# Two transformer layers in one kernel: zero rows by ScalarE, bias adds by GpSimd, and a reordered load queue

## The reference

```python
x = L0_attn_x                                # (4, 256, 512) f32
xn = _layernorm(x)
x = x + attn0(xn) + gelu(xn @ W1 + fc1_bias) @ W2 + fc2_bias             # hidden 2048
xn = _layernorm(x)
x1, x2 = split(xn @ w12.T + b12)                                         # hidden 512
x = x + causal_attn1(xn) + (silu(x1) * x2) @ w3.T + b3                   # 32 heads, 8 key heads of 16
```

## Time and profile before

| quantity | value |
| --- | --- |
| median of 3 runs (lowest, highest) | 619.87 us (619.39, 623.91) |
| the profiled execution | 624.43 us |
| its span, first to last instruction | 622.3 us |
| mean granted PE clock | 0.981 of full speed |
| first transpose, first maximum matmul, first score on PE | 9.70, 35.22 and 46.83 us into the span |
| ACT's first square root (L855) | 7.78 us |
| POOL's last memset or mask ends | 27.2 us |
| PE's wait ahead of the first up product | 25.7 to 29.4 us |
| DVE's last work ahead of 542 us ends | 540.0 us |
| layer 0 / layer 1 border (unit 16's first scores) | about 390 us |
| busy share of PE, DVE, ACT, POOL | 93%, 73%, 57%, 35% |
| bytes moved by DMA | 67.29 MB, 108 GB/s mean |

### The profile page before, as it was taken

One profiled execution on the slowest core, in us unless ns is written; L12 is line 12 of the kernel. 1 busy time (PEld: TensorE's weight loads), 2 busy tenths in 40 slices (PEclk: granted clock), 3 DMA queues, 4 the chain that ended last, 5 costly groups with the idle time before them and its releaser, 6 DMA issues.

```text
span 622.3 us, 10485 instructions
## 1 busy us (share of the span) xinstructions
PE 577.9 (93%) x3232; PEld 443.3 (71%) x3232; DVE 451.5 (73%) x1198; ACT 356.0 (57%) x611; POOL 217.8 (35%) x332
## 2 busy tenths in 40 slices
PE   2698899999999999999999998899989989899997
PEld 2686677787777878667777777677767877666754
DVE  6559967656566675576897677889997988578663
ACT  3337766755555683676694575657655654465541
POOL 5712423122303321211223122354644555254241
PEclk9999899999999999999999999989999999988989
DMA  5583542353223244315443332425433344334101
GB/s 186 176 241 127 141 115 67 105 153 103 68 86 103 70 131 124 86 45 160 120 136 101 95 90 74 120 85 139 141 98 102 86 127 130 87 102 116 23 5 63
DMA packets 29806, 67.29 MB, mean 108 GB/s; under 512 B 4788, under 2 KB 17588, under 8 KB 27704
## 3 DMA queue, kind: packets, MB, share of 16 engines
q1 hardware_dynamic: 21112, 38.32, 22.2%
q0 software_dynamic: 8640, 28.32, 15.6%
HBM read 51.67 MB, written 14.68 MB: 107 GB/s over the span
## 4 chain that ended last, share of the span: by engine, by line
PE 73%; DVE 9%; ACT 6%; issue 5%; DMA 5%; POOL 1%; SPq 1%; ACTq 0%; DVEq 0%; POOLq 0%
PE banks L692 49%; PE banks L745 8%; PE banks L771 7%; PE banks L793 7%; DMA q_sb<-q_parts 2%; DVE banks L1065 1%; DMA q_sb<-max_t 1%; ACT L910 1%; PE banks L774 1%; PE banks L712 1%; ACT hid_f L930 1%; ACT L929 1%; DVE bn L976 1%; ACT probs L910 1%; DVE x_res L1109 1%
## 5 line engine op out<-in xcount | busy, mean ns | idle before, releaser
L910 ACT ACTIVATE probs<-banks 128x512 f32<-128x512 f32 (+1 forms) x256 | 137.6, 545 | 185.1 <-PE banks L771 143.9
L692 PE MATMUL banks<-xnT,w_up 128*128 128x512 f32 x576 | 154.7, 403 | 5.4 <-issue 3.8
L1070 DVE TENSOR_REDUCE neg_max<-banks 128x2 f32<-128x512 f32 x128 | 87.1, 687 | 93.2 <-PE banks L745 92.6
L692 PE MATMUL banks<-w_down,hid 128*128 128x512 f32 x480 | 131.1, 407 | 4.5 <-ACT hid_f L930 2.0
L692 PEld LDWEIGHTS banks<-xnT,w_up 128*128 128x128 f32 x576 | 103.4, 192 | 33.9 <-issue 15.1
L1065 DVE CUSTOM_DVE_ANT_0 banks<-banks,mask_qk 128x128 f32<-128x128 f32 (+1 forms) x256 | 86.3, 374 | 39.4 <-PE banks L745 39.4
L692 PEld LDWEIGHTS banks<-w_down,hid 128*128 128x128 f32 x480 | 87.7, 193 | 32.3 <-DVE neg_max L1070 6.7
L745 PEld LDWEIGHTS banks<-k_sb,q_sb 96*128 96x128 f32 x512 | 93.7, 193 | 23.3 <-issue 5.2
L745 PE MATMUL banks<-k_sb,q_sb 96*128 96x256 f32 (+1 forms) x512 | 100.8, 279 | 5.2 <-DMA q_sb<-q_parts 4.0
L648 POOL TENSOR_SCALAR_AFFINE_SELECT probs<-probs 128x256 f32<-128x256 f32 x128 | 59.6, 466 | 102.6 <-ACT probs L910 97.5
L771 PE MATMUL banks<-q_sb,k_sb 97*128 97x512 f32 x192 | 79.9, 416 | 8.8 <-ACT probs L910 6.9
(11 more groups left out here) (77 smaller groups left out, 651.3 us busy)
## 6 DMA issues: line engine op xcount, KB each, us to landing
q_sb<-q_parts SPq DMA_DIRECT2D x64, 256.0 KB, 4.4
raw<-in_up POOLq DMA_DIRECT2D x48, 256.0 KB, 3.0
raw<-in_down POOLq DMA_DIRECT2D x40, 256.0 KB, 3.1
q_parts<-stage SPq DMA_DIRECT2D x32, 256.0 KB, 2.5
raw<-in_attn POOLq DMA_DIRECT2D x20, 256.0 KB, 3.2
k_parts<-stage SPq DMA_DIRECT2D x16, 256.0 KB, 2.6
k_sb<-k_parts SPq DMA_DIRECT2D x16, 256.0 KB, 4.0
x_res<-in_x SPq DMA_DIRECT2D x4, 512.0 KB, 4.0
```

Source lines behind the costliest of these rows:

```text
L692: mm = nc.tensor.matmul(out_ap, lhs(a), rhs(b_), start=first and j == 0, stop=stop and j == 2, **kw)
L910: nc.scalar.activation(probs[:, i, 0:w], banks[:, ST_BANKS[k % 2], 0:w], ACT.Exp, scale=SCALES[n // B]).then_inc(exp_done, 1)
L1070: nc.vector.tensor_reduce(neg_max[:, s, 2 * g:2 * g + 2, t], banks[:, bank_of[x], :].rearrange("p (r t) -> p r t", r=2)[:, :, 0:w], AX.X, ...
```

## The change

Six edits are made together.

1. POOL no longer zeroes q_sb; three ACT copies from a zero column do (`fill`). Two stand ahead of everything else on ACT, the third behind the second batch's transposes. POOL's other memsets are put in another order, and its raw loads no longer alternate with them.
2. The first batch of x is loaded as two DMAs of 256 KB, one for each tile.
3. The key loads (`load_k`) of batch 0 go behind the first query store on SP.
4. The three output biases are now laid out as 128 x 512 arrays each and loaded by three DMAs of 256 KB instead of two of 8 KB. POOL sums two of them once (`bias`).
5. The sixteen bias matmuls are gone. Sixteen POOL additions of bias_out to a tile of x_res (`plus`) take their place: six in unit 3, two in each of units 7, 11, 15, 19 and 23. The DVE additions of products to x_res stay.
6. Each `out` stands behind the next `mrow` instead of right behind the tile's last product.

```diff
 def start_slots():
-    o = [[("stats", 0, 0), ("root", 0, 0), ("rstd", 0, 0), ("ln", 0)] + split(0, "attn", 4, 5)]
+    o = [[("fill", 0), ("fill", 1), ("stats", 0, 0), ("root", 0, 0), ("rstd", 0, 0), ("ln", 0)] + split(0, "attn", 4, 5)]
     o += [[("xn", 0, 0), ("xn", 0, 1)] + split(0, "attn", 0, 1)]
...
     o += [parts(("qkv", 0, 2)) + split(0, "attn", 2, 3)]
-    o += [parts(("qkv", 0, 0)) + [("load_k", 0, 0), ("load_k", 0, 1)]]
-    o += [[("xn", 1, 0), ("xn", 1, 1), ("load_q", 0), ("load_q", 1)] + split(0, "up", 0, 1)]
+    o += [parts(("qkv", 0, 0))]
+    o += [[("xn", 1, 0), ("xn", 1, 1), ("fill", 2), ("load_k", 0, 0), ("load_k", 0, 1), ("load_q", 0), ("load_q", 1)] + split(0, "up", 0, 1)]
     o += [parts(("qkv", 0, 1)) + [("v", 0)]]
...
         slots[7].append(("rstd", 1, c))
+    if s == 3 and n + 2 < 2 * B:
+        for c in ((0, 1, 2) if n == 0 else (n + 2,)):
+            slots[2 if n else 2 * c].append(("plus", c // B, TT * (c % B)))
+            slots[4 if n else 2 * c + 1].append(("plus", c // B, TT * (c % B) + 1))
     if s == 2 and n + 2 < 2 * B:
...
         k = max(k for k, x in enumerate(o) if adds_to(x) == (1, tile))
-        o.insert(k + 1, ("out", tile))
+        rows = [j for j, x in enumerate(o) if j > k and x[0] == "mrow"]
+        o.insert((rows[0] if rows else k) + 1, ("out", tile))
     return o
...
         return x[1] // B, TT * (x[1] % B) + x[2]
+    if x[0] == "plus":
+        return x[1], x[2]
...
         bias_up = sb("bias_up", [P, 24])
-        bias_out = sb("bias_out", [P, 2, D], F32R)
-        ones = sb("ones", [P, P], F32R)
+        bias_out = sb("bias_out", [P, 2, D])
+        zero = sb("zero", [P, 1])
...
-        bias_raw = probs[:, 6:8, :]
+        bias_more = probs[:, 7, :]
...
 
-            eng.wait_ge(wk_emptied, em[x if x[0] == "wo" else ("down",) + x[1:]] + 1)
+            if x[0] == "plus":
+                eng.wait_ge(plus_done, pls[x] + 1)
+            else:
+                eng.wait_ge(wk_emptied, em[x if x[0] == "wo" else ("down",) + x[1:]] + 1)
 
...
 
-        IDENT, Q_ZERO, ONES_V, ZEROED, ALL_MADE, EARLY = 2, 7, 8, 9, 12, 9
+        IDENT, K_ZERO, ONES_V, ALL_MADE, EARLY = 3, 4, 5, 8, 4
 
...
 
-            load_x(0)
+            for t in range(TT):
+                sp_.dma_start(x_res[:, t, :], x_in[0][t * P:t * P + P, :]).then_inc(x_loaded[0] if t else x_first, 16)
             sp_.wait_ge(raw_loaded[1], 16)
...
                 if x[0] == "load_bias":
-                    sp_.wait_ge(made, ZEROED)
-                    for row in (0, 32):
-                        sp_.dma_start(bias_raw[row:row + 2, :, :], out_b).then_inc(bias_loaded, 16)
+                    for k, to in enumerate((bias_out[:, 0, :], bias_out[:, 1, :], bias_more)):
+                        sp_.dma_start(to, out_b[k]).then_inc(bias_loaded, 16)
                 if x[0] == "store":
...
 
+            nc.gpsimd.memset(zero[:, :], 0.0).then_inc(made, 1)
+            pool.wait_ge(made, 1)
             load(0)
...
             nc.gpsimd.memset(ident[:, :], 0.0).then_inc(made, 1)
-            pool.wait_ge(made, 1)
+            pool.wait_ge(made, 2)
             nc.gpsimd.affine_select(out=ident[:, :], in_=ident[:, :], compare_op=ALU.not_equal, fill=1.0,
...
             pool.wait_ge(made, IDENT)
+            nc.gpsimd.memset(k_sb[64:ROWS, :, :].bitcast(F32), 0.0).then_inc(made, 1)
+            pool.wait_ge(made, K_ZERO)
             pool.wait_ge(x_loaded[0], 16)
...
             load(3)
-            nc.gpsimd.memset(k_sb[64:ROWS, :, :].bitcast(F32), 0.0).then_inc(made, 1)
-            pool.wait_ge(made, 3)
-            load(4)
-            load(5)
-            nc.gpsimd.memset(k_sb[MROW:MROW + 1, :, :].bitcast(F32), 1.0).then_inc(made, 1)
-            pool.wait_ge(made, 4)
-            for k in range(RING):
-                load(6 + k)
-                nc.gpsimd.memset(q_sb[64:ROWS, k, :, :].bitcast(F32), 0.0).then_inc(made, 1)
-                pool.wait_ge(made, 5 + k)
             nc.gpsimd.memset(v_sb[:, :, :, :], 1.0).then_inc(made, 1)
             pool.wait_ge(made, ONES_V)
-            nc.gpsimd.memset(bias_raw[:, :, :], 0.0).then_inc(made, 1)
-            pool.wait_ge(made, ZEROED)
-            nc.gpsimd.memset(ones[:, :].bitcast(F32), 1.0).then_inc(made, 1)
-            pool.wait_ge(made, 10)
+            nc.gpsimd.memset(k_sb[MROW:MROW + 1, :, :].bitcast(F32), 1.0).then_inc(made, 1)
+            pool.wait_ge(made, ALL_MADE - 2)
             nc.gpsimd.memset(mask_qk[:, :], 0.0).then_inc(made, 1)
-            pool.wait_ge(made, 11)
+            pool.wait_ge(made, ALL_MADE - 1)
             nc.gpsimd.affine_select(out=mask_qk[:, P:], in_=mask_qk[:, P:], compare_op=ALU.is_ge, fill=MASKED,
...
                     done[0] = (mask_done, st_index(u - LU, i) + 1)
+                if x[0] == "bias":
+                    pool.wait_ge(bias_loaded, 48)
+                    in_order()
+                    nc.gpsimd.tensor_tensor(bias_out[:, 1, :], bias_out[:, 1, :], bias_more, ALU.add).then_inc(bias_summed, 1)
+                    done[0] = (bias_summed, 1)
+                if x[0] == "plus":
+                    _, L, tile = x
+                    n, t = B * L + tile // TT, tile % TT
+                    pool.wait_ge(ln_done, TT * n + t + 1)
+                    if add_before[x]:
+                        wait_tile_sum(pool, add_before[x])
+                    in_order()
+                    nc.gpsimd.tensor_tensor(x_res[:, tile, :], x_res[:, tile, :], bias_out[:, L, :], ALU.add).then_inc(plus_done, 1)
+                    done[0] = (plus_done, pls[x] + 1)
                 if x[0] == "ctx":
...
                     k = work(x)
-                    if x == ("m", 0, 0):
-                        pe.wait_ge(made, Q_ZERO)
+                    if u < RING and i == 0:
+                        pe.wait_ge(made, K_ZERO)
+                        pe.wait_ge(q_zeroed, u + 1)
                     if i == 0:
...
                     k = work(x) if opens else bank_of[x]
-                    if opens and rest == 0:
-                        pe.wait_ge(bias_split, 1)
-                        nc.tensor.matmul(banks[:, k, :], ones[:, :], bias_out[:, L, :],
-                                         start=True, stop=False, skip_group_check=True)
                     if opens:
...
                         mm = three(banks[:, k, :], lambda h: hid[:, c % HID, h, t * P:t * P + P],
-                                   lambda h: w_down[:, c % 2, h, :], rest > 0 and e == 0, e == 1, skip_group_check=True)
+                                   lambda h: w_down[:, c % 2, h, :], e == 0, e == 1, skip_group_check=True)
                     if closes:
...
                     nc.scalar.copy(to[0], raw[:, k % RAW, :]).then_inc(hi_split, 1)
+                if x[0] == "fill":
+                    act.wait_ge(made, 1)
+                    nc.scalar.copy(q_sb[64:ROWS, x[1], :, :].rearrange("p g t -> p (g t)"),
+                                   zero[64:ROWS, :].to_broadcast([ROWS - 64, UH * T])).then_inc(q_zeroed, 1)
                 if x[0] == "root":
...
                     act.wait_ge(st_filled, k + 1)
-                    if k == 6:
-                        act.wait_ge(bias_split, 1)
+                    if k == 7:
+                        act.wait_ge(bias_summed, 1)
                     if u:
...
                         if L == 0:
-                            dve.wait_ge(x_loaded[t // TT], 16)
+                            dve.wait_ge(x_loaded[t // TT] if t else x_first, 16)
                         else:
...
                                             ALU.add).then_inc(rot_done, 1)
-                if x[0] == "bias":
-                    dve.wait_ge(bias_loaded, 32)
-                    link(nc.vector.tensor_copy(bias_out[:, :, :], bias_raw[:, :, :]))
-                    nc.vector.tensor_tensor(bias_out[32:64, :, :], bias_raw[32:64, :, :],
-                                            bias_out[32:64, :, :].bitcast(F32), ALU.subtract).then_inc(bias_split, 1)
                 if x[0] == "v":
...
                         nc.vector.transpose(o_t[:, :], o_div[:, :]).then_inc(o_back, 1)
-                if adds_to(x):
+                if adds_to(x) and x[0] != "plus":
                     tile = adds_to(x)[1]
...
     up_b = np.concatenate([i["L0_ffn_fc1_bias"].reshape(-1, P), i["L1_ffn_b12"].reshape(-1, P)]).T
-    zero = np.zeros(D, np.float32)
-    out_b = np.stack([np.stack([i["L0_ffn_fc2_bias"], i["L1_ffn_b3"]]), np.stack([zero, i["L1_attn_b_dense"]])])
+    out_b = np.stack([np.broadcast_to(b, (P, D)) for b in (i["L0_ffn_fc2_bias"], i["L1_ffn_b3"], i["L1_attn_b_dense"])])
     inv = (np.float32(1.0) / np.power(np.float32(1e6), np.arange(0, HD, 2, dtype=np.float32) / np.float32(HD))).astype(np.float32)
```

6 lines of the change are left out of this document (5 added, 1 removed).

## The result

The changed kernel took **614.2 us** (median of four runs, 611.85 to 617.68) against 621.62 us for the kernel before, measured beside it (four runs, 619.39 to 623.91). The ratio is 0.9869, 95% interval 0.9833 to 0.9906: 1.3% faster, 8 us by the ratio (the two medians lie 7.4 us apart). Its profiled execution took 612.6 us, with a span of 610.8 us, 11.5 us shorter than the 622.3 us of before; 9.9 us were forecast for that pair. The two profiled executions differ in their clock too. Before had a mean granted clock of 0.981 and after one of 0.989, so full clock was withheld for 11.8 us of the first span (0.019 of 622.3) and 6.7 us of the second.

A forecast was written before the change was run, and what follows sets the result against it. PE, busy for 577.9 of 622.3 us, was taken to bound the kernel, apart from a few waits. Terms 2.9 + 1.0 + 2.4 + 3.0 + 0.6 - 1.5 gave 8.4 us, 611.5 us from 619.87, range 605 to 617.

The forecast's parts named there:

- The start: Up to the first maximum matmul: the query store moves up, gaining 2.9 us, bounds 0.5 and 5 us.
- the first rival: Start gives nothing back: wait moves ahead of the maxima, clock falls, bias loads delay the first row; 615.4 us, 22%.
- Unit 0: Bias operations off DVE gain 1.5 us, less 0.5 for the bias loads: net 1.0 us.
- the 0.5 for the bias loads: In unit 0, 768 KB of loads ahead of the first row of maxima: loss between 0 and 2 us, 0.5 taken.
- Bias matmuls: Sixteen fewer on PE at 0.23 us each, ten or eleven counted: 2.4 us gained, bounds 1.2 and 3.7.
- The stall: PE's wait and slow clock around 542 us end: 4.5 us in the profiled execution, 3.0 us in the median.
- The limit that I expected of DVE: At the stall near 542 us, DVE, busy until 540.0 us, was to become the limit at once.
- the row of maxima at 502 us: An output's issue at 501.68 us stood ahead of a row PE waits for: 0.6 us gained.
- POOL's additions: About 1.3 us each, four showing in units 19 and 23: a loss of 1.5 us, bounds 0 and 21.9.

The follow-up runs named there:

- e4: The changed kernel without POOL's sixteen additions of the output biases, which its output then lacks; ratio 0.9855 to the kernel before.
- e11: The changed kernel with the three bias loads moved behind the first row of maxima, nothing else; 609.76 us, ratio 0.9808 to the kernel before.
- e2: The changed kernel with the output biases back on PE as sixteen matmuls, with DVE's splits and the small bias loads; ratio 0.9921 to the kernel before.
- e5: The kernel before with only the outputs moved behind the next row of maxima; 618.85 us, ratio 0.995 to the kernel before.
- e3: The changed kernel with each output again right behind the step that finishes its tile; ratio 0.9925 to the kernel before.
- e6: The changed kernel with thirteen extra matmuls, their result unread, filling PE's wait ahead of the first maxima; ratio 0.9884 to the kernel before.
- e7: The changed kernel with the second up product of layer 0 moved into PE's wait ahead of the maxima; ratio 0.9861 to the kernel before.
- e9: The changed kernel with only unit 0's key half and query buffer loaded behind the first query store, the others after the second; ratio 0.9835 to the kernel before.
- e8: e7 with ACT's fills moved, POOL's last memsets behind the layer norm and bias loads behind the first row of maxima; ratio 0.9837 to the kernel before.
- e10: e8 with the order of loads of e9; 609.52 us, ratio 0.9794 to the kernel before.
- e1: The changed kernel with the old start: one first-batch load, POOL's q_sb memsets, key loads ahead of the query store; ratio 0.9905 to the kernel before.
- e12: The changed kernel with the edits of e7 and e11 together; ratio 0.9833 to the kernel before.

## Why the prediction was right

The total was right: 611.5 us forecast, range 605 to 617, measured 614.2. As a gain that is 1.36% forecast and 1.3% measured, since the kernel before came out 1.75 us slower beside the changed one than the 619.87 that the forecast started from. The mechanism of the steps held except for the end of the start; four sizes were off, in both directions.

- **The start** was booked at 2.9 us. The times were right to the tenth up to the maxima: store 22.1 for 22.3, first maximum matmul 32.34 for 32.3, no gain for the first batch. But the wait moved ahead of the maxima and the clock fell there, the half of the first rival that I had bounded by 0.5 us and not taken: 1.4 us were left at the first score. The low clock isn't the whole account, however: in e4, the same program up to there, it stayed full and the late row of maxima behind the bias loads took as much. Both halves of the rival were true, and either is enough. e11 shows the full term, 3.4 us, where neither holds.
- **Unit 0** was booked at 1.0 and brought 2.6, of which 0.5 come without edits 4 and 5 too (e2, e5). DVE gave 1.88, its whole share and more than my 1.5; the 0.5 for the bias loads did not show in the changed kernel, since PE was late for the row anyway; at full clock they are some 1.4 us (PE's wait for the row in e4, none in e11).
- **Bias matmuls**, 2.4: the price of 0.25 us was right, the count was not. Only the four of unit 8 are seen as a step, 1.0 us. Of the four in unit 0 the last, at 66.15 us, stands in the chain of before and is some 0.2 of unit 0's 2.6; the others don't show. The eight of layer 1 show nothing beyond the spread (e2, e5). With the start this is the term that was furthest off.
- **The stall**, 4.5 in the profiled execution and 3.0 in the median: 6.0 and about 3.1 (e5). The limit that I expected of DVE did not bind: PE is busy for all of 534 to 540 us. That the median would miss part of it held. For the row of maxima at 502 us I booked 0.6 us; the step from unit 23 to 24 is 0.75 us shorter in the changed kernel, 0.28 in e3 with the old outputs and 0.55 in e5 with that edit alone, so some 0.5 are the edit's.
- **POOL's additions**, -1.5: measured 1.3 us each as said, and they cost 0.6 at most in all. The Trainium skill, page "SBUF — State Buffer", section "SBUF: two separate sides", would by my estimate have made it 5.2 us if four were met at their start; e4 rules that out. The rows of the start do fit an exclusive lock held to the end of POOL's operation: rs, which began inside POOL's memset, ends 0.03 us behind it.
- **Not foreseen**: 1.1 us given back in unit 17, taken up below; and 1.84 us near the end, in unit 31, where twelve matmuls (two groups of six) took 4.16 us in the chain of before (from 602.77 us) and 2.76 in that of after. Neither is taken to be of the change: e11, with the same program there, has no low clock in unit 17, and one from 587.0 to 590.4 us that costs it 1.55 of these 1.84.

As sums, the trace of after has 1.4 + 2.6 + 1.0 + 6.0 against my 2.9 + 1.0 + 2.4 + 4.5: 11.0 for 10.8. Start and bias matmuls were booked 2.9 us too high, unit 0 and the stall 3.1 us too low. That the total came out right is luck: the errors cancel.

## What to carry to other kernels

Where a start is bound by transfers, price the next transfer before you move the last one: e4, e6, e7 and e9 left the maxima at full clock and lost it to a row that landed late, and e8 issued its query load 3.5 us earlier and lost that to a load that took longer. e10 kept it with the needed load put first and the bias loads behind the row. Where two limits stand at the same place, removing one shows nothing, and that isn't evidence that it cost nothing. Work that an engine can do without its late input belongs into its wait. An order of DMA issues that puts a store with a late condition ahead of a load can be seen in the queue alone; mending it alone gave 3.1 us here (e5). Extra instructions of the busiest engine cost only where the chain runs through it: count them there, not over the kernel.

## What the runs showed of the hardware

**The same wait lowered PE's clock in one execution and not in the next.** In unit 17 PE waits for ACT ahead of its first score. The timeline of the changed kernel and then of e11:

```profile
399.57 0.79 PE L792 MATMUL banks<-q_sb,k_sb 97*128 97x512 f32 x1 [2.69 <-ACT probs L931]
```

```profile
397.19 0.50 PE L792 MATMUL banks<-q_sb,k_sb 97*128 97x512 f32 x1 [2.68 <-ACT probs L931]
```

The next six 512-column matmuls took 2.56 us in the first (chain of waits) and 1.39 us in the second. The granted clock of the first is 0.50 from 398.8 to 405.6 us. The chain of the first:

```profile
399.57 0.79 PE banks L792
400.36 0.43 PE banks L766 x2
400.79 2.56 PE banks L712 x6
```

Before had the low clock in unit 17 as well, but for half as long, 405.1 to 408.5 us. Stretch, before:

```profile
405.20:408.40 3.20, 3.20 (x15) 1.79 (x14) 3.12 (x7) 0.60 (x1) 2.51 (x3) 0.50 0.31 82
```

That is why after gives 1.1 us back against before, and e11, with none, gains 1.5. All fourteen traces have this wait, 2.67 to 2.69 us long. In ten of them a low clock began between 0.8 us ahead of the score and 1.5 us behind it; in e5, e8, e10 and e11 none did. Ahead of the maxima, waits of 2.68 (e2), 3.04 (after), 3.12 (e10), 3.19 (e1), 3.54 (e3) and 6.07 us (e8) were followed or met by the low clock; in the six traces with 0.63 to 2.28 us there and no long wait earlier (e4, e6, e7, e9, e11, e12) it stayed full.

**The run's time follows its clock.** Each such place is worth 1 to 2 us, and the mean granted clock was taken for every run. The four runs of the changed kernel have spans of 610.0 us at 0.992, 610.8 at 0.989, and 614.0 and 615.9 at 0.983. Of the runs of before beside e1 to e4, the two at 0.994 have 615.7 and 617.0 us, and one at 0.978 has 624.1. So most of the spread between runs of one kernel goes with the clock, and two profiled executions are best compared with their clocks beside them.

**One load, 5.0 or 10.6 us.** The same query load took 4.99 us issued at 26.72 us (changed kernel, DMA share 0.93 from 22 to 34 us) and 10.63 issued 3.5 us earlier (e8), closer behind the key loads, at a DMA share of 1.02. The row of maxima, 8 KB, took 2.1 to 5.4 us.

**POOL's memset holds a small DVE operation to its end**: 1.77 and 1.82 us (before) and 1.11 us (after) in place of 0.17, each time ending within 0.04 us of the memset's end.
